# Graph network on one core: a block's messages copied from PSUM by ScalarE and added to the sums by GpSimd

## The reference

```python
Wh = h @ W + b
sim = dot(Wh[row], Wh[col]) / (norm(Wh[row]) * norm(Wh[col]))
base = adj_v * softplus(deg_coeff[0] * deg_v + deg_coeff[1]) * (row != col)
prop_pos = segment_sum((base * relu(sim))[:, None] * Wh[col], row)
prop_neg = segment_sum((base * -relu(-sim))[:, None] * Wh[col], row)
out = scale * (coeff[0] * prop_pos + coeff[1] * prop_neg + coeff[2] * Wh)
```

## Time and profile before

| what | value |
|---|---|
| median of three runs | 1071.21 us |
| the profiled execution's own time | 1065.46 us |
| its span | 1063.8 us |
| mean granted TensorE clock | 0.934 |
| TensorE busy | 850.4 us (80%) |
| VectorE busy | 902.9 us (85%) |
| ScalarE busy | 583.1 us (55%) |
| GpSimd busy | 170.9 us (16%) |

### The profile page before, as it was taken

One profiled execution on the slowest core, in us unless ns is written; L12 is line 12 of the kernel. 1 busy time (PEld: TensorE's weight loads), 2 busy tenths in 40 slices (PEclk: granted clock), 3 DMA queues, 4 the chain that ended last, 5 costly groups with the idle time before them and its releaser, 6 DMA issues. The chain is left out here.

```text
span 1063.8 us, 33473 instructions
## 1 busy us (share of the span) xinstructions
PE 850.4 (80%) x14240; PEld 596.1 (56%) x14240; DVE 902.9 (85%) x1310; ACT 583.1 (55%) x1994; POOL 170.9 (16%) x316
## 2 busy tenths in 40 slices
PE   0596558877888878887878888755999998999997
PEld 0362435544455444554544545425999998996653
DVE  8977979999999999999999989856666798587896
ACT  0764546666676665666665756517999942112000
POOL 4814801121111211112211111100000000000000
PEclk9888669999999999999998989966999999997999
DMA  8933214543444434445334435549700000783893
GB/s 197 222 135 82 64 51 112 126 125 95 108 113 119 133 95 113 109 108 137 102 95 110 111 95 126 145 142 395 287 2 2 3 1 1 309 301 134 316 394 125
DMA packets 39321, 144.66 MB, mean 136 GB/s; under 512 B 13476, under 2 KB 14070, under 8 KB 35446
## 3 DMA queue, kind: packets, MB, share of 16 engines
q1 hardware_dynamic: 33990, 133.22, 42.3%
q0 software_dynamic: 2912, 7.92, 2.9%
q10 hardware_dynamic: 2256, 1.23, 0.5%
HBM read 78.63 MB, written 63.72 MB: 134 GB/s over the span
## 5 line engine op out<-in xcount | busy, mean ns | idle before, releaser
L1135 PE MATMUL b_ps<-b_mv,b_soh 64*128 64x50 bf16 (+1 forms) x9600 | 190.7, 190 | 111.1 <-DVE b_mv L1024 69.5
L1135 PEld LDWEIGHTS b_ps<-b_mv,b_soh 64*128 64x128 bf16 x9600 | 164.0, 95 | 161.6 <-DVE b_mv L1024 110.0
L1355 PE MATMUL layers_ps<-layers_u,layers_c 128*128 128x192 bf16 x2500 | 212.4, 248 | 11.8 <-ACT layers_u L1537 9.2
L1355 PEld LDWEIGHTS layers_ps<-layers_u,layers_c 128*128 128x128 bf16 x2500 | 209.4, 99 | 17.1 <-DVE layers_y L1661 8.0
L927 ACT ACTIVATE b_c_row<-b_ps 128x300 bf16<-128x300 f32 (+1 forms) x275 | 117.1, 426 | 83.9 <-PE b_ps L1135 78.7
L945 ACT ACTIVATE b_pos<-b_ps,k_coef 128x1024 f32<-128x1024 f32 x100 | 92.7, 927 | 125.4 <-PE b_ps L1135 118.5
L1024 DVE TENSOR_TENSOR b_mv<-b_mv,b_parts 128x2808 bf16<-128x2808 bf16 x100 | 147.9, 1479 | 0.0
L1062 DVE TENSOR_TENSOR b_y<-b_sim,b_ps 128x512 f32<-128x512 f32 (+1 forms) x175 | 109.7, 627 | 34.8 <-PE b_ps L1189 29.0
L1546 ACT ACTIVATE k_passed<-layers_c 128x128 bf16<-128x128 bf16 x450 | 131.4, 293 | 0.0
L1020 DVE TENSOR_TENSOR b_soh<-k_numbers,b_bits 128x2304 bf16<-128x2304 bf16 x100 | 121.9, 1219 | 0.0
L1135 PE MATMUL b_ps<-b_unit,b_wh_b 64*128 64x512 f32 (+1 forms) x350 | 102.5, 629 | 8.8 <-ACT b_fld L913 6.8
(11 more groups left out here) (272 smaller groups left out, 1065.6 us busy)
## 6 DMA issues: line engine op xcount, KB each, us to landing
layers_c<-g_blocks SPq DMA_DIRECT2D x25, 1600.0 KB, 9.0
g_blocks<-b_g_row SPq DMA_DIRECT2D x52, 400.0 KB
c_blocks<-b_c_row SPq DMA_DIRECT2D x25, 800.0 KB, 4.4
g_blocks<-head_odd SPq DMA_DIRECT2D x48, 400.0 KB, 4.3
layers_c<-c_blocks SPq DMA_DIRECT2D x12, 1600.0 KB, 26.9
prep_attr<-in_edge_attr SPq DMA_DIRECT2D x2, 1883.0 KB
prep_attr<-in_edge_attr SPq DMA_DIRECT2D x1, 1876.0 KB
rec<-sort_rec SPq DMA_DIRECT2D x1, 1209.0 KB, 4.5
```

The source lines that it names most:

```text
L1135: return nc.tensor.matmul(out, lhsT, rhs, start=start, stop=True, skip_group_check=True)
L1355: return nc.tensor.matmul(out_, lhsT, rhs, start=start, stop=True, skip_group_check=True)
```

## The change

For the first 24 of the 25 messages, VectorE's four adds are gone. In their place ScalarE copies each piece from PSUM to a new SBUF tile `sent` ([128, 3 x 512 + 128] fp32) at four places of its list: piece 0 after lot 4, piece 1 after lot 8, pieces 2 and 3 after props 5 and 6 (`LEAVE`). These copies now raise `added`, on which TensorE waits. GpSimd adds the tile to the sums in two instructions (128 x 1536 and 64 x 128) at the end of its step, once all four pieces are copied; `summed` tells ScalarE that the tile is free again. The last message stays on VectorE. GpSimd also doubles part 1 of a block one step earlier, ahead of the new adds. This holds for the first round alone; the code for graphs of more rounds (`again`) does not run with these inputs and is left as it was, save that its tile `scale` now lies in `sent`.

```diff
+BYSUM = NB - 1
...
+LEAVE = [("lot", 4), ("lot", 8), ("prop", 5), ("prop", 6)]
...
-        sim, scale = [l.sb(f"sim{i}", [P, 1024]) for i in range(2)], l.sb("scale", [P, 512])
+        sent = [l.sb(f"sent{i}", [P, 3 * 512 + P]) for i in range(1)]
+        sim, scale = [l.sb(f"sim{i}", [P, 1024]) for i in range(2)], sent[0][:, 0:512]
...
+            def message(v):
+                pool.wait_ge(s["added"], NG * v + NG + 1)
+                for here, sent_ in ((k["passed"][:, 0:NG - 1, :].rearrange("p g n -> p (g n)"), sent[0][:, 0:3 * 512]),
+                                    (k["passed"][0:F, NG - 1, 0:P], sent[0][0:F, 3 * 512:3 * 512 + P])):
+                    nc.gpsimd.tensor_tensor(here, here, sent_, ALU.add).then_inc(s["summed"], 1)
...
                 if early:
+                    double(1, 1, 1)
                     gather(4, 11, 13)
...
-                for o in range(1, 4):
+                for o in range(2 if isinstance(w, int) else 1, 4):
                     double(w, b, o)
                 if not (isinstance(b, int) and b == NB - 1):
                     double(w + 1, b + 1, 0)
+                    if isinstance(w, int):
+                        double(w + 1, b + 1, 1)
+                if isinstance(w, int):
+                    message(b - 1)
...
+            def send(v, g):
+                m, n = (P, 512) if g < NG - 1 else (F, P)
+                act.wait_ge(s["propped"], NC * v + (2 * NC + 1 + min(2 * g + 2, NC)))
+                if v >= 1 and g == 0:
+                    act.wait_ge(s["summed"], 2 * v)
+                bank = PR if g < NG - 1 else AT
+                nc.scalar.activation(sent[v % 1][0:m, 512 * g:512 * g + n], ps[0:m, bank, 0:n], ACT.Copy).then_inc(s["added"], 1)
...
                     if what == "sims":
                         positive(w - 1, i)
+                    if isinstance(w, int) and w <= BYSUM:
+                        for g in range(NG):
+                            if (what, i) == LEAVE[g]:
+                                send(w - 1, g)
...
             def add(v, g):
                 m, n = (P, 512) if g < NG - 1 else (F, P)
+                if isinstance(v, int) and v < BYSUM:
+                    return
                 dve.wait_ge(s["propped"], NC * v + (2 * NC + 1 + min(2 * g + 2, NC)))
+                if isinstance(v, int) and v == BYSUM and g == 0:
+                    dve.wait_ge(s["summed"], 2 * BYSUM)
```

More of the change, by code:

```diff
@@ L715, in build @@
         s = {n: l.sem(n) for n in names.split()}
-        s_win, s["further"] = k["win"], k["further"]
+        s_win, s["further"], s["summed"] = k["win"], k["further"], k["summed"]
         s_stored = [l.sem(f"stored{i}") for i in range(2)]
@@ L1878, in four_layers @@
         k["rows"], k["win"] = [top.sem(f"rows{g}") for g in range(len(GATES))], [top.sem(f"win{g}") for g in range(len(GROUPS))]
-        k["further"], k["starts"] = top.sem("further"), top.sem("starts")
+        k["further"], k["starts"], k["summed"] = top.sem("further"), top.sem("starts"), top.sem("summed")
         table = top.sb("table", [1, 2], I32)
```

## The result

The changed kernel takes 1124.82 us (median of 4 runs, 1117.62 to 1126.20), the kernel before 1070.18 us on the same chip. The ratio is 1.048 (95% interval 1.043 to 1.052): slower by 55 us. The forecast was 33 us slower, 1104 us. The profiled execution took 1126.2 us with a span of 1124.5 us, 61 us more than that of before; its mean granted clock is 0.898 against 0.934.

A forecast was written before the change was run, and what follows sets the result against it. It took mv 1's end and ScalarE's time from there to lot 5's end to bound a block; 23 x 0.82 plus 24 x 0.59 gave 33 us more, 1104 us. Its own range was 1083 to 1130, the whole range 1065 to 1135.

The forecast's parts named there:

- VectorE's busy share is no bound by itself and a second chain lies close behind: VectorE, busy 21.22 of 21.86 us a block, waits for TensorE 0.16 us before y 4, 0.31 before y 6.
- GpSimd's add and the one-hots exclude each other, and where the add falls: GpSimd's add waits for mv 0, ends at 6.38 and holds off hi 1; mv 1 ends 0.82 us later.
- The estimate of 3.3 us for the add by twice the copy's slope: GpSimd's 128x1536 add: two inputs through one path at 1.0 ns an element each, plus 0.2, giving 3.3 us.
- ScalarE's copy ahead of lot 5, 0.59 us: ScalarE's copy of piece 0 between lots 4 and 5 delays lot 7 and turn 4 by 0.59 us a block.
- From there TensorE and ScalarE run by themselves: From lot 3, after mv 1, through lot 5's emptying, TensorE and ScalarE proceed without VectorE; no size given.
- The low clocks before: Granted clock in the kernel before: 0.86 noted for the block of 25.24 us, with no term in the sum.
- The last rival: GpSimd's long add gets in ahead of mv 0, mv 1 about 2.9 us later: 1152 us; chance 0.12.
- No change: GpSimd's add is short or does not hold VectorE; ScalarE's 0.59 eats the 0.45 gained: 1074 us; chance 0.17.
- faster: As no change, and lot 7 does not wait for the delayed lot 5: 1060 us, up to 1023; chance 0.11.
- the bounds of the add's length: GpSimd's long add: 1.4 us gives +3 us in all; 4.1 us with all small ones gives +79 us.

The follow-up runs named there:

- run 1: The changed kernel with GpSimd's two adds cut to one column each; 1060.88 us, ratio 0.990 to the kernel before.
- run 8: Changed kernel, GpSimd's add in four pieces a step later where VectorE has one SBUF input, ScalarE's copies of pieces 0, 1 behind props 1, 3; 1048.23 us.
- run 4: Kernel before plus a long GpSimd add on its own tile, part 1 doubled ahead of it, the add released ahead of mv 0; 1119.76 us.
- run 6: Changed kernel with ScalarE's copies of pieces 0 and 1 behind props 1 and 3 instead of lots 4 and 8; 1106.95 us.
- run 5: Changed kernel with 12 fp32 matmuls of ones into a free bank in TensorE's wait before lot 3; 1089.61 us.
- run 10: Kernel before with 5 fp32 matmuls of ones into the free bank ahead of lot 3; 1054.28 us.
- run 3: Kernel before plus a long GpSimd add on its own tile behind mv 0, with part 1 doubled ahead of the add; 1086.85 us.
- runs 2: Kernel before plus a long GpSimd add on its own tile behind mv 0, part 1 not doubled earlier; 1141.41 us.

## Why the prediction was right or wrong

- *That VectorE's busy share is no bound by itself and a second chain lies close behind.* Right: with the adds gone and nothing held off (run 1) the beat is 21.95 us, not 19.9, which is 21.86 - 0.41 + 0.49, the working of the forecast without the add.
- *That GpSimd's add and the one-hots exclude each other, and where the add falls.* Right in place and size. The add ended at 6.41 (6.38), hi 1 was ready at 5.47 (5.41), mv 1 ended 0.78 later (0.82). The estimate of 3.3 us for the add by twice the copy's slope was right: 4.61 - 1.29 = 3.3, and from the 1.27 us of a 128x512 add (run 8) to this it is 2.0 ns an element. The Trainium skill's 4497 ns for 2048 elements ("GPSIMD Engine Reference", Performance versus the Vector engine) gave 3.4 as an estimate, and the measured 3.3 is close to that too.
- The Trainium skill's rule in "SBUF — State Buffer", Who interferes with whom, that the first to issue keeps the shared path for the whole instruction: the trace agrees in both directions (1.62 instead of 0.23 us on GpSimd, 1.20 instead of 0.40 and, in run 4, 4.17 instead of 1.61 on VectorE).
- *ScalarE's copy ahead of lot 5, 0.59 us.* Right, 0.49; run 6 takes it away. The step from start to start was 0.47.
- *"From there TensorE and ScalarE run by themselves."* This is the step that failed. I carried TensorE's durations over from the block before unchanged, though I had made its wait ahead of them longer (from 1.53 to 2.4 us in my own sum). Behind the longer wait it ran at the lower clock, which cost 1.43 us in every block and 1.24 more in every third. With it the sum comes out: 23 x 0.78 + 24 x 0.49 + 23 x 1.43 + 8 x 1.24 = 72 us, less the 15 us by which the nine longer blocks of the kernel before exceed 21.86, is 57; the 23 distances together grew by 58. And with the wait filled (run 5) the beat is 23.3 us, the one forecast.
- *The low clocks before.* I named one, 0.86 in the block of 25.24 us, and gave it no price. That row would have misled: in this block lot 3 follows its wait of 1.53 us at full speed, and the slow stretch comes later, behind one of the gaps. Those that would have told are the five blocks at 0.93. The first two rows are from one of them, the others from the block of 25.24 us:

```profile
420.68 0.71 PE L1135 MATMUL b_ps<-b_mv,b_soh 64*128 64x75 bf16 x36 [1.53 <-DVE b_mv L1024]
...
422.17 1.97 PE L1135 MATMUL b_ps<-b_y,b_u_b 128*64 128x512 f32 x4
```

```profile
603.94 0.71 PE L1135 MATMUL b_ps<-b_mv,b_soh 64*128 64x75 bf16 x36 [1.53 <-DVE b_mv L1024]
...
612.49 0.59 PE L1189 MATMUL b_ps<-k_ident,b_a_row 128*128 128x128 f32 x3 [0.83 <-issue]
613.01 1.98 PE L1135 MATMUL b_ps<-b_y,b_u_b 128*64 128x512 f32 x4
```

- *The last rival* (the add gets in ahead of mv 0) did not happen, but run 4 made it happen. *No change* and *faster*: the holding off was in every block. Run 1 shows what they would have been. Its beat, 0.09 us longer than before, is that of *no change* (0.14), where ScalarE's copy eats what was gained; its time, 1061 us, is lower than the 1074 named there, with the higher clock.
- The time lay inside the range by luck: the range had been drawn for the bounds of the add's length, not for the clock.

## What to carry to other kernels

Before moving work from VectorE to GpSimd, list which VectorE instructions read two SBUF tensors, and put the GpSimd work beside the others, in pieces that fit: the same four adds cost 55 us as one block and gave 12 us cut in pieces and placed, 22 with ScalarE's copies moved as well. And when a change makes TensorE wait longer, price the stretch behind the wait at the lower clock as well; a few matmuls into an unused bank during the wait were worth 35 us here (run 5), and 17 us in the kernel before (run 10).

## What was not expected of the hardware

A wait of 2.6 us ahead of lot 3 was followed by slow matmuls in all 23 blocks (the changed kernel), one of 1.85 us in 21 (run 3), one of 1.53 us in four of 22 (before; its one wait of 1.82 us was followed by them too), and one of 1.46 or 1.47 us in none of 22 (run 8). What sets those four blocks apart is not shown. A gap of 0.8 to 1.2 us with nothing waited for was followed by a slow stretch in some blocks (before, 612.49) and not in others (run 8, 227.25). A GpSimd add with one tile as both inputs and output took 3.1 to 3.3 us together with its small one (runs 2 and 3), where the add of two different tiles took 3.3 by itself.
